# Two attention layers and two expert layers on one core: the first batch's queries and keys reach their rows by 0/1 products instead of a trip through memory

## The reference

```python
q = q * cos + rotate_half(q) * sin          # layer 0; layer 1: q, k, v = proj(...)
scores = jnp.einsum('bqhd,bkhd->bhqk', q, k) * scale + bias[None]   # 16 heads of 16
attn = jax.nn.softmax(scores, axis=-1)
out = jnp.einsum('bhqk,bkhd->bqhd', attn, v)
...
x = x + _L0_xattn_ref(_layernorm(x, axis=-1), ctx_1024, ctx_1024, 16)
...
x = x + _L1_xattn_ref(_layernorm(x, axis=-1), ctx_1024, ctx_1024, ...)
```

## Time and profile before

| | us |
|---|---|
| median of 3 runs (lowest, highest) | 1135.06 (1132.0, 1137.83) |
| the profiled execution, its own time | 1133.8 |
| its span, first to last instruction | 1132.0 |
| attention, layer 0: first maxima, first scores, step 8, end | 48.3, 74.0, 104.3, 280.3 |
| attention, layer 1: start, first maxima, first scores, step 8, end | 510.1, 582.6, 607.9, 644.7, 857.2 |
| busy: PE, DVE, ACT, POOL | 921.2, 601.9, 508.7, 335.3 |

### The profile page before, as it was taken

How to read it: one execution, slowest core, us unless ns; L and a number is a source line. 1 busy time by engine, 2 the same in 40 slices (tenths; PEclk the granted TensorE clock), 3 DMA queues, 4 the chain that set the end, 5 groups by cost and what they waited for, 6 DMA issues and landing times. The chain is left out here.

```text
span 1132.0 us, 16721 instructions
## 1 busy us (share of the span) xinstructions
PE 921.2 (81%) x6514; PEld 612.6 (54%) x6514; DVE 601.9 (53%) x993; ACT 508.7 (45%) x766; POOL 335.3 (30%) x317
## 2 busy tenths in 40 slices
PE   0269989898989999982758998999985339999994
PEld 0123334343989999970424444444434329999994
DVE  7768969782541111105035675768715545665553
ACT  1127767677203333320224676667661205554550
POOL 5575833001012222211543322200000344455322
PEclk9999989999889999995787999989996559999997
DMA  9968363300248999956296518060006214345516
GB/s 164 232 197 198 89 154 83 64 5 2 83 173 296 331 352 343 334 200 168 111 188 178 122 58 142 31 115 4 3 2 221 80 56 112 112 131 162 136 19 167
DMA packets 50994, 159.06 MB, mean 141 GB/s; under 512 B 7664, under 2 KB 27888, under 8 KB 40240
## 3 DMA queue, kind: packets, MB, share of 16 engines
q1 hardware_dynamic: 36720, 123.80, 38.7%
q0 software_dynamic: 14208, 34.35, 12.0%
HBM read 116.31 MB, written 40.76 MB: 139 GB/s over the span
## 5 line engine op out<-in xcount | busy, mean ns | idle before, releaser
L767 DVE TENSOR_REDUCE a_row_max<-ps_ring 128x2 f32<-128x1024 f32 x256 | 308.9, 1222 | 145.0 <-PE ps_ring L577 143.7
L700 ACT ACTIVATE a_probs<-ps_ring 128x1024 f32<-128x1024 f32 x256 | 261.0, 1023 | 105.4 <-PE ps_ring L592 103.3
L611 PE MATMUL ps_out<-a_probs,a_vaug 128*32 128x256 f32 x2048 | 168.7, 403 | 2.5 <-ACT a_out_sb L706 1.5
L577 PE MATMUL ps_ring<-a_ka,a_qa 52*128 52x512 f32 (+1 forms) x512 | 120.6, 475 | 56.3 <-DMA a_ka<-scratch_k_scr 48.9
L592 PE MATMUL ps_ring<-a_qa,a_ka 56*128 56x512 f32 (+1 forms) x512 | 132.4, 514 | 8.2 <-DMA a_qa<-a_max_t 5.4
L592 PEld LDWEIGHTS ps_ring<-a_qa,a_ka 56*128 56x128 f32 (+1 forms) x512 | 49.2, 189 | 103.5 <-issue 68.3
L952 ACT ACTIVATE e_hid<-ps_ring,e_wts 128x128 f32<-128x128 f32 x184 | 52.4, 370 | 110.1 <-PE ps_ring L1021 75.6
L577 PEld LDWEIGHTS ps_ring<-a_ka,a_qa 52*128 52x128 f32 (+1 forms) x512 | 52.1, 202 | 88.8 <-issue 38.8
L1369 PE MATMUL ps_ring<-e_xt,e_wr 128*128 128x512 f32 x384 | 90.2, 394 | 2.7 <-DVE e_xt L1437 2.7
L1308 ACT ACTIVATE e_hr<-ps_ring 128x512 fp32r<-128x512 f32 x64 | 38.3, 599 | 117.6 <-PE ps_ring L1369 117.6
L1021 PEld LDWEIGHTS ps_ring<-e_xst,e_wts 128*128 128x128 f32 x736 | 85.7, 192 | 2.0 <-issue 0.8
(11 more groups left out here) (210 smaller groups left out, 1217.8 us busy)
## 6 DMA issues: line engine op xcount, KB each, us to landing
e_wts<-in_w SPq DMA_DIRECT2D x23, 1156.0 KB, 7.8
e_wts<-in_w SPq DMA_DIRECT2D x23, 1024.0 KB, 7.7
e_wf<-in_w SPq DMA_DIRECT2D x16, 1024.0 KB, 5.3
scratch_k_scr<-a_kst POOLq DMA_DIRECT2D x18, 512.0 KB, 12.4
scratch_q_scr<-a_qst POOLq DMA_DIRECT2D x36, 256.0 KB, 3.2
a_qa<-scratch_q_scr SPq DMA_DIRECT2D x24, 384.0 KB, 11.5
a_ka<-scratch_k_scr SPq DMA_DIRECT2D x24, 384.0 KB, 13.6
a_ctx_t<-in_ctx_t SPq DMA_DIRECT2D x8, 512.0 KB, 8.5
```

What stands on the lines that cost most here:

```text
L577: ins = pe.matmul(to[:, par], qa[rows, b % 2, g, p, qt * P:(qt + 1) * P], ka[rows, b % 2, g, p], start=True, stop=True)
L611: ins = pe.matmul(m.ps_out[VW * h:VW * (h + 1), cols], vaug[:, b % NV, kc, HG * g + h], probs[:, t % 3, h, cols], start=(kc == 0 and half ...
L700: nc.scalar.activation(probs[:, t % 3, 2 * half:2 * half + 2], unit("s", n), ACT.Exp, scale=HD ** -0.5).then_inc(exp_done, 1)
L767: dve.tensor_reduce(row_max[:, s % 3, qt, :, p], unit("m", n), AX.X, ALU.max).then_inc(mx_read, 1)
```

## The change

- **First batch.** Batch 0 is neither stored nor loaded. TensorE multiplies the split parts by 0/1 matrices (`marks`, in the unused second half of `ka`, filled by `mark`), which sends each channel to its row, into a ring unit of 1024 columns: four pairs of heads, keys and queries, so eight spreadings (`spread_keys`, `spread_queries`). A last product brings in bias and selection rows in layer 0 (`last_rows`, `table`). ScalarE copies each unit to `ka` or `qa` (`spread_rows`), VectorE half of the first two. The first two stand before step -8, the others by `SPREAD_AT` behind steps -8, -7, -6, -3, -1 and 1. Batch 1's splits wait for all eight (`spread` at 8), since they write the same `kst` and `qst`.
- **Idle products.** `keep_awake` issues products of the identity whose results nobody reads: 14, 26 and 4 in layer 0; 30, 16, 8 and 4 in layer 1.
- **Maxima.** `load_max` moves from SyncE to ScalarE's queue, behind the copy it reads.
- **Order.** Statistics are made per batch 0, batch 1, and within steps 0 to 6 for batches 2 and 3. Batch 0's rounding moves to ScalarE, both its rotations to VectorE. `normed` is split into one tile per step. The jobs of `first` use two banks in turn; in layer 1 only batch 0's stand there, and those of the others, and the queries, stand later. Layer 1's first projection waits for five constants instead of seven. Constant rows for the second half wait for the eighth spreading.

```diff
+SPREAD_AT = {-8: ("k", 1), -7: ("q", 1), -6: ("k", 2), -3: ("q", 2), -1: ("k", 3), 1: ("q", 3)}
+AWAKE_AT = ({("q", 0): 14}, {("qt", 0): 16})
...
-        q_at = {i: (-7, -5)[i % 2] if i < 4 else 16 * (i // 2) - (30, 26)[i % 2] for i in range(2, 2 * B)}
+        first = [("k", 0, 0), ("k", 0, 1), ("v", 0, 0), ("v", 0, 1), ("qt", 0), ("qt", 1), ("q", 0), ("q", 1)]
+        q_at = {i: (-2, 0)[i % 2] if i < 4 else 16 * (i // 2) - (24, 20)[i % 2] for i in range(2, 2 * B)}
...
+        for job, t in ((("k", 1, 0), -6), (("k", 1, 1), -3), (("v", 1, 0), 2), (("k", 2, 0), 6), (("v", 1, 1), 7), (("k", 2, 1), 10), (("v", 2, 0), 11),
+                       (("k", 3, 0), 14), (("k", 3, 1), 15), (("v", 2, 1), 18), (("v", 3, 0), 30), (("v", 3, 1), 33)):
+            put(job, t, 0)
...
         def split_keys(eng, chain, b):
             if b == 1:
-                eng.wait_ge(k_first, 48)
+                eng.wait_ge(spread, 2 * NG)
...
-            if 2 <= i < 4:
-                eng.wait_ge(q_first, 96)
-            elif i >= 4:
+            if i < 4:
+                eng.wait_ge(spread, 2 * NG)
...
-                            if t == (2 if b == 1 else 16 * b - 14) + 2 * part:
+                            if t == (6 + part if b == 1 else 16 * b - 14 + 2 * part):
                                 load(b, part)
-                    for job in ended.get((t, 1), []):
-                        if job[0] == "m":
-                            load_max(job[1])
...
+                for par in range(2):
+                    pool.wait_ge(spread, 2 * NG)
+                    if layer == 0:
+                        constant_rows(par, ka, QK_ROWS, "k_bias", 1)
+                        constant_rows(par, qa, QK_ROWS, "q_bias", 1)
+                    constant_rows(par, ka, M_ROWS, "k_select", 1)
...
+                def keep_awake(n):
+                    for _ in range(n):
+                        pe.matmul(ring[:, 5, 0:P], m.ident[:], m.ident[:], start=True, stop=True)
...
+                def spread_keys(g):
+                    if g == 0:
+                        pe.wait_ge(k_ready, 1)
+                        pe.wait_ge(marks_set, 2 - layer)
+                    to = take_unit("k", g)
+                    for p in range(PAIR):
+                        h = PAIR * g + p
+                        for c in range(DC):
+                            at = MARK - P - HD // 2 * c
+                            pe.matmul(to[:, p], hi_k[:, h, at:at + P], kst[:, 0, c], start=(c == 0), stop=False, skip_group_check=True)
+                            ins = pe.matmul(to[:, p], one_row[:, h, at - 2 * HD:at - 2 * HD + P], kst[:, 1, c], start=False, stop=(layer == 1 and c == DC - 1), skip_group_check=True)
+                        if layer == 0:
+                            ins = pe.matmul(to[:, p], last_rows[:, 0, h], table[:, 0], start=False, stop=True, skip_group_check=True)
+                    ins.then_inc(spread, 1)
...
                         nc.scalar.copy(max_t[:, s % 2], misc[0:2 * MAX_ROWS]).then_inc(misc_free, 1)
+                        load_max(s)
...
+                def spread_rows(kind, g):
+                    dst, n_to = (ka, S_ROWS if layer == 0 else M_ROWS) if kind == "k" else (qa, M_ROWS)
+                    act.wait_ge(spread, 2 * g + (1 if kind == "k" else 2))
+                    for par in range(1 if g == 0 else 2):
+                        rows = slice(par * HALF_P, par * HALF_P + n_to)
+                        ins = nc.scalar.copy(dst[rows, 0, g], unit(kind, g)[rows])
+                    ins.then_inc(spread_act, 1)
...
                     for i in range(2, 2 * B):
-                        if t == max(q_at[i] - 3, steps[0]):
-                            normed(i)
+                        if t in (q_at[i] - 2, q_at[i] - 1):
+                            normed(i, [t - q_at[i] + 2])
...
+                norms(range(TB, 2 * TB))
+                for n, (kind, dst, n_rows_to) in enumerate((("k", ka, S_ROWS if layer == 0 else M_ROWS), ("q", qa, M_ROWS))):
+                    dve.wait_ge(spread, n + 1)
+                    rows = slice(HALF_P, HALF_P + n_rows_to)
+                    dve.tensor_copy(dst[rows, 0, 0], unit(kind, 0)[rows]).then_inc(spread_dve, 1)
                 for t in steps:
+                    if 0 <= t < 4:
+                        ins = tile_stats(range(2 * TB + 2 * t, 2 * TB + 2 * t + 2))
...
+                    if t == 6:
+                        norm_scale(range(2 * TB, NT))
```

More of the change, by code:

```diff
@@ L201, in attention @@
         consts_in = sem("consts_in")
-        rows_in = sem("rows_in")
+        rows_in = [sem("rows_in0") if layer == 1 else None, sem("rows_in1")]
         ctx_in = [sem(f"ctx_in{i}") for i in range(2)]
@@ L206, in attention @@
         q_ready = sem("q_ready")
-        k_first = sem("k_first")
-        q_first = sem("q_first")
+        late_in = sem("late_in") if layer == 1 else None
+        table_in = sem("table_in") if layer == 0 else None
+        marks_zero = sem("marks_zero")
+        others_zero = sem("others_zero") if layer == 0 else None
+        marks_set = sem("marks_set")
+        turned = sem("turned") if layer == 0 else None
+        rounded = sem("rounded") if layer == 0 else None
+        spread = sem("spread")
+        spread_act = sem("spread_act")
+        spread_dve = sem("spread_dve")
         k_stored = sem("k_stored")
@@ L231, in attention @@
         ring = m.ps_ring
-        n_const = 2 if layer == 0 else 7
+        n_const = 2 if layer == 0 else 5
         n_ctx = 2 if layer == 0 else 1
         n_rows = 6 if layer == 0 else 2
+        n_first = len(first)
+        MARK = P + 2 * HD + DC * HD // 4
+        marks = ka[:, 1].rearrange("p g a t -> p (g a t)")
+        others = qa[:, 1].rearrange("p g a t -> p (g a t)")
+        one_row, hi_k, hi_q = (marks[:, n * H // 2 * MARK:(n + 1) * H // 2 * MARK].rearrange("p (h m) -> p h m", m=MARK) for n in range(3))
+        last_rows = others[:, 0:H * P].rearrange("p (a h m) -> p a h m", a=2, m=P)
+        table = others[:, H * P:H * P + 2 * T].rearrange("p (a t) -> p a t", a=2)
         k_scr = dram["k_scr"]
@@ L586, in scores @@
                     b, g = s // NG, s % NG
+                    if n == 0 and layer == 1:
+                        pe.wait_ge(rows_in[0], 16 * n_rows)
                     if kc == 0 and p == 0:
```

330 lines of the change are left out of this document (213 added, 117 removed).

## The result

The changed kernel takes 1221.5 us (median of 4 runs, 1200.1 to 1241.7) against 1133.5 for the kernel before (4 runs, 1127.8 to 1137.8). The ratio is 1.0645, with a 95% interval of 1.0584 to 1.0707; it rests on the two shorter runs (1200.1 and 1217.4, median 1208.7), since the other two (1225.7 and 1241.7) lie over 1.5% above the shortest and are set aside.

A forecast was written before the change was run, and what follows sets the result against it. TensorE waits at both layers' starts; behind step 8 three engines follow closely, so added ScalarE time costs in full. Terms sum to +29.6 on 1133.8, so 1163 us; range 1110 to 1180.

The forecast's parts named there:

- (a): Loop behind step 8: two maxima transfers hold ScalarE 1.33 us in each of 26 groups, +34.6 us.
- (d): Loop behind step 8: waits for maxima caused by SyncE's queue, and the lower clock behind them, go, -9 us.
- (e): Loop: one tile normalised per step costs about half of the 1.18 us hold, 8 times 0.6, -5 us.
- start of layer 1: From layer 1's start to step 8: first maxima at 544.3, step 8 at 619.8 against 644.7, -24.9 us.
- Start of layer 0: Up to step 8 of layer 0: wait for batch 1's rows moves there, step 8 at 116.8 against 104.3, +12.5 us.
- rival C: Idle products don't hold the clock, spreadings up to step 1 run at the lower level: 1176 us; chance 0.12.
- signs of being wrong: Plain groups still 11.7 us, no wait for rows at step 8 (about 20 and 5 us), or first maxima over 8 off.
- (c): Step 8 of each layer: TensorE waits, then starts at the lower clock level, 2.2 us each, +4.4.
- rival A: ScalarE's issue of the maxima transfers is nearly free, the 34.6 us go: 1129 us; chance 0.20.
- Rival B: Batch 1's rows are in time, step 8 at 97 and 615: 1134 us; chance 0.12, with A 0.11.
- (b): Layer 1 behind step 8: four more key and value jobs at 2.0 and two query jobs at 3.7; one in layer 0: +17 us.

The follow-up runs named there:

- experiment 1: Changed kernel with only the transfers of the maxima put back on SyncE's queue: 1168.1 us, ratio 1.0295.
- experiment 7: Kernel before, layer 1's last two constants on their own semaphore 1121.0; plus one tile a step 1121.3, or six later jobs 1125.2, or re-ordered key jobs 1117.9.
- Experiment 5: Changed kernel with SyncE transfers and earlier statistics (1161.2): batch 1's stores issued by SyncE, 1174.8; or batch 1's queries not rotated in layer 0, 1160.0.
- experiment 2: Kernel before: both maxima transfers on ScalarE 1220.4; one transfer 1149.1; or ScalarE held by a copy of 1408 columns 1186.6, of 1664 columns 1208.0.

## Why the prediction was wrong

The step that failed first is term (a): it priced the transfers on ScalarE as a hold alone, 34.6 us, and put the lower clock of TensorE behind each gap at nothing. The runs showed 53.7 in the two loops. Next to it the gains (d) and (e), 14 us together, did not come, and the start of layer 1 was taken 10.9 too short. The sum was + 12.5 - 24.9 + 34.6 + 17 + 4.4 - 9 - 5. Its parts, in its order:

- **Start of layer 0: right, in part by luck.** First maxima at 32.5 (34.4 forecast), first scores at 64.8 (62.4), the eighth spreading ends at 75.8 (72.8), GpSimd's row lasts 26.6 (27.9), step 8 at 117.3 (116.8). The eighth spreading 3.0 late was made up by a row 1.3 and a landing 1.2 shorter (117.3 - 102.5 = 14.8, for 16.1). VectorE's small operations took up to 1.2 us each beside GpSimd's rotation. The wait was not one of 20 us on the rows but 7.0, with 6.9 ahead of it for the statistics, which I had not seen, and which cost nothing extra here.
- **Start of layer 1: 10.9 too good** (-14.0, not -24.9). First maxima came 40.9 us after the end of the experts (40.0 forecast). But the eight steps of the prologue took 36.8 us for the 29 I had put in. The clock was at 0.86 there (0.84 in layer 0), which is rival C's mechanism; but some 10 us at the lower level, at a third to a half lost, are 3 to 5 of the 7.8, and what the rest is was not looked into. Then ScalarE waited for the statistics here too, 6.9 us, with 5.5 for TensorE. The wait of 5 us for the rows at step 8, one of my signs of being wrong, did not come: TensorE itself was late.
- **(a), the transfers on ScalarE: 34.6 forecast, 53.7 measured** in the loops of the profiled executions (40 by the ratios), and 4.6 more in the expert stage behind it (230.2 us, and 225.6 in the version of experiment 1), which no run explains. This is the largest miss. The hold is as forecast, 1.33 to 1.36 us, and the gaps make 26 groups at most 1.54 longer, 40 us. What I left out is that TensorE's clock falls behind such a gap; I had priced that for the two waits at step 8, in (c), and not for 26 gaps of 1.5 us. The Trainium skill (Perfetto Trace Analysis, DMA Instruction — HWDGE) says that the sequencer is free at the end of the reported span; the trace agrees, with 1.47 us from the first issue to the exponential (833.28 to 834.75), and rival A, by which the issue is nearly free, is dead: 0.31 of my chance stood on it, alone or with B.
- **(b) to (e): 7.4 forecast, 25.0 measured**, by the loops of experiment 1: 182.2 - 174.4 = 7.8 in layer 0 and 217.2 - 200.0 = 17.2 in layer 1. The gains in it did not come. (d), 9 us for the maxima that SyncE sent late: they wait as long with ScalarE's queue, 7.3 us against 5.4. It was not SyncE's queue that made them late. (e), one tile a step: no gain seen in experiment 7. (b), the jobs: 2.7 us for a key or value job and not 2.0, as experiment 7 shows; the copies between the products count too.
- **Rival B** (batch 1 in time) did not come. Experiment 5 showed that even with GpSimd's row 7.7 us shorter step 8 moves by 3.4 only.

These add up: 0.5 + 10.9 + 19.1 for the queue (53.7 by the loops, less 34.6) + 17.6 + 5.5 for the expert stages = 53.6, and 83.6 - 29.6 = 54.0.

## What to carry to other kernels

In a loop where three engines follow one another without slack, a hold on one can cost twice: the gap, and what TensorE's clock does behind it. Price both, and look for the hold's length: 0.7 us a group cost 14 us here, 1.5 us a group cost 85. An early start is worth only what the next thing is in time for; here the rows of batch 1 took back what batch 0 had won, and the cheapest two edits, a semaphore that isn't waited for and an order of jobs, gave more than the whole re-ordering. Where a term rests on who is to blame for a wait, as (d) did, it is worth no more than that blame is shown.

## What the runs showed of the hardware

- TensorE's granted clock fell to its lower level (1.2 GHz) behind many, not all, of the gaps of 1.5 us that come every 13 us or more, when it was otherwise busy: within 4 us its products took 0.79 behind 16 of 20 such gaps (both transfers, experiment 2), behind 13 of 19 of 1.4 to 1.6 us, and behind 8 of 20 of 1.2 to 1.4. With gaps of 0.85 us in such groups, a few of 1.0 to 1.2 among them, it stayed at 2.4 GHz throughout (1.00).
- At the lower level a half step of this loop takes 2.16 us instead of 1.46, not twice as long. The exponential in it takes 1.02 us at either level.
- A VectorE operation on 8 columns took 3.60 us (it takes 0.17) and ended with GpSimd's addition of 1024 columns (2.35 us from 652.16), VectorE first:

```profile
650.94 3.60 DVE L79 SCALAR_TENSOR_TENSOR a_tmp<-a_tmp 128x8 f32<-128x8 f32 x1
```
```profile
649.96 2.18 POOL L282 DMA_DIRECT2D scratch_q_scr<-a_qst  x3 [0.30 <-POOL a_qst L329]
...
652.16 2.35 POOL L492 TENSOR_TENSOR x_res<-x_res,a_bo 128x1024 f32<-128x1024 f32 x1
```

It began while GpSimd was issuing transfers and went on through the addition. The Trainium skill (SBUF — State Buffer, Who interferes with whom) calls the shared port an exclusive lock, and this agrees with it in that the operation ended with the addition. But it had started 1.2 us ahead of the addition, so who came first does not explain it, and no row tells what held it until then.
